# The first FFN group's work placed inside the last entry of the attention before it

## What is computed

```python
x = x + L0_xattn(ctx_1024, layernorm(x), mask)      # 8 heads of 64; q from x, k and v from context and x; l2norm of q and k
x = x + L0_ffn(layernorm(x))                        # up to 3 steps: relu(x Wm) Wp on the active quarter, top-k router
x = x + L1_xattn(layernorm(x), ctx_1024, ctx_1024)  # 16 heads of 8
x = x + L1_ffn(layernorm(x))                        # latent attention, then a mixture of 8 experts
```

## Time and profile before

| | us |
|---|---|
| median of three runs | 1278.69 |
| lowest, highest | 1275.88, 1280.52 |
| the profiled execution, whole | 1280.42 |
| its span, first to last instruction | 1278.9 |

### The profile page before, as it was taken

The page is one execution under the profiler, slowest core; times in us unless marked ns, Lnnn a source line. Parts: engine busy times, 40 slices in busy tenths (PEclk is TensorE's granted clock), DMA queues, the critical chain, the costliest instruction groups (busy, mean ns, idle before and its releaser), DMA issues.

```text
span 1278.9 us, 38214 instructions
## 1 busy us (share of the span) xinstructions
PE 1221.2 (95%) x13719; PEld 874.3 (68%) x13719; DVE 936.8 (73%) x2049; ACT 797.5 (62%) x2101; POOL 585.1 (46%) x675
## 2 busy tenths in 40 slices
PE   4899999999999995998999999999999989999996
PEld 1566666666666664447888788788888767777774
DVE  7767766777667764579999999999999965344331
ACT  2687788878877783225877787767666733333331
POOL 5476666566665663414333423353233234333442
PEclk9999999999999998998999999999999999999998
DMA  9000000000000000000000002000000000000000
GB/s 225 14 2 2 0 0 0 0 0 0 0 0 0 1 1 5 0 0 12 10 10 10 11 8 72 3 4 1 0 0 0 1 1 9 9 8 8 8 16 10
DMA packets 22742, 14.74 MB, mean 12 GB/s; under 512 B 6378, under 2 KB 21610, under 8 KB 22540
## 3 DMA queue, kind: packets, MB, share of 16 engines
q1 hardware_dynamic: 22520, 13.75, 4.3%
q10 hardware_dynamic: 148, 0.01, 0.0%
HBM read 11.66 MB, written 2.10 MB: 11 GB/s over the span
## 4 chain that ended last, share of the span: by engine, by line
PE 40%; issue 10%; POOL 5%; DVE 3%; POOLq 0%; ACT 0%; DVEq 0%
PE psum L1580 10%; PE psum L1591 5%; PE psum L1567 5%; POOL pair_acc L2310 4%; PE psum L1594 4%; PE psum L998 2%; PE psum L2090 2%; PE psum L2100 2%; PE psum L1005 2%; PE psum L1562 2%; PE psum L1546 1%; PE psum L1548 1%; PE psum L1547 1%; PE psum L1602 1%; POOL pair_acc L2304 1%
## 5 line engine op out<-in xcount | busy, mean ns | idle before, releaser
L715 POOL TENSOR_TENSOR r_norm<-ssm,mhalf 128x24 f32<-128x24 f32 x32 | 134.9, 4215 | 156.9 <-DVE ssm L619 156.8
L1948 POOL TENSOR_TENSOR pair_QX<-pair_qT,own_slots 128x512 f32<-128x512 f32 x64 | 66.6, 1040 | 248.4 <-ACT pair_qT L1679 236.0
L2156 ACT ACTIVATE pair_hid<-psum 128x512 f32<-128x512 f32 x128 | 76.4, 597 | 141.3 <-PE psum L2090 141.3
L1580 PE MATMUL psum<-ident,pair_probs 128*120 128x128 f32 (+1 forms) x1024 | 153.9, 283 | 0.4 <-ACT pair_probs L1694 0.2
L541 ACT ACTIVATE l_probs<-psum,l_n_max 128x248 f32<-128x248 f32 x256 | 117.2, 482 | 57.9 <-DVE l_n_max L637 57.9
L2310 POOL TENSOR_TENSOR pair_acc<-pair_acc,pair_prod 128x512 f32<-128x512 f32 x64 | 81.2, 1269 | 140.0 <-DVE pair_prod L2269 140.0
L1694 ACT ACTIVATE pair_probs<-psum,pair_n_max 128x120 f32<-128x120 f32 (+1 forms) x512 | 137.7, 380 | 10.8 <-DVE pair_n_max L1748 5.7
L2100 PEld LDWEIGHTS psum<-w,pair_hid 128*128 128x128 f32 x1024 | 123.1, 192 | 26.8 <-issue 26.8
L2269 DVE TENSOR_TENSOR pair_prod<-psum,pair_combine 128x512 f32<-128x512 f32 x64 | 44.2, 691 | 129.7 <-PE psum L2100 129.5
L1515 ACT COPY pair_probsT<-psum 120x512 f32<-120x512 f32 (+1 forms) x128 | 78.7, 615 | 84.7 <-PE psum L1580 84.7
L1580 PEld LDWEIGHTS psum<-ident,pair_probs 128*120 128x120 f32 (+1 forms) x1024 | 109.4, 140 | 31.1 <-ACT pair_probs L1694 12.3
(11 more groups left out here) (294 smaller groups left out, 2922.9 us busy)
## 6 DMA issues: line engine op xcount, KB each, us to landing
X<-x_in SPq DMA_DIRECT2D x8, 256.0 KB, 6.2
out_dram<-pair_acc SPq DMA_DIRECT2D x32, 64.0 KB, 1.5
CT<-ctx_in SPq DMA_DIRECT2D x8, 240.0 KB, 6.6
pair_cT<-ctxT_in SPq DMA_DIRECT2D x32, 60.0 KB, 1.8
w<-w_in SPq DMA_DIRECT2D x1, 1024.0 KB, 5.4
wm<-wm_in SPq DMA_DIRECT2D x1, 768.0 KB, 7.3
wp<-wp_in SPq DMA_DIRECT2D x1, 768.0 KB, 8.7
wkv<-wkv_in SPq DMA_DIRECT2D x1, 512.0 KB, 5.0
```

The costliest lines, as they stand in the source:

```text
L715: pool.tensor_tensor(r_norm[:, :], ssm[:, :], mhalf[:, 0:3 * H], ALU.pow).then_inc(s["norm_inverted"], 1)
L1580: tr = pe.transpose(psum[0:K, 4 + g % 2, j * P:(j + 1) * P], probs[par][:, 4 * g + j, 0:K], ident[:, :])
```

## The change

- Four `up` products, the first `down` product and the transposes (`turn_in`) of FFN group 0 stand between the steps of entry 31 of the first attention, on PE; ACT's and DVE's share of it (`copy_in`, `relu`, `load_in`, `activate`) in their bodies 30 and 31.
- Behind PE's last body `finish_first` stands: the other three `down` products of group 0, `turn_in` of group 1 and its first two `up` products. ACT copies in group 1 and copies out group 0. With that the Block ends.
- Mean and variance of entries 0 to 27 are made by DVE in body 30, the inverse roots by POOL in bodies 30 and 31. Those of entries 28 to 31 are made in the FFN's Block (`last_scales`), where DVE waits for POOL's inverse root behind group 1.
- `prepare_ffn` and its Block are gone. The joining of the weights stands on PE and ACT between the FFN and the second attention (`join_weights`), filling `history` in POOL's `make_constants`, `l1_bias` and `index` in `last_scales`. The FFN's loop on PE and DVE starts with group 2.
- `down` adds up in PSUM bank 3 in place of bank 4, since the attention uses bank 4. The context is loaded to X3, a tile that is free until the FFN writes it, in place of CT; the FFN's tiles are made ahead of the attention.

```diff
-        sem = sems.enter_context(signals(nc, "l0"))
-        CT = sb("CT", [P, B, D])
...
                 def body(n, par):
+                    last = isinstance(n, int) and n == B - 1
                     values_x(n + 1)
                     scores(n, 1, par)
                     project(n - 1)
+                    if last:
+                        pe.wait_ge(s["klT_copied"], B)
+                        pe.wait_ge(s["vc_copied"], B)
+                        ffn["turn_in"](pe, 0)
                     turn_inputs(n + 2)
                     turn_probs0(n, 0)
                     turn_probs1(n, 0)
+                    if last:
+                        pe.wait_ge(later_weights_loaded, 16 * len(later_weights))
+                        pe.wait_ge(ffn["in_copied"], 1)
+                        ffn["up"](pe, 0, 0)
                     project_kc(n + 2)
                     turn_sums(n, 0)
                     project_q(n + 2)
                     multiply_v(n, 0, par)
+                    if last:
+                        ffn["up"](pe, 0, 1)
                     turn_probs0(n, 1)
                     turn_kc(n + 1)
                     project_kl(n + 2)
                     turn_probs1(n, 1)
+                    if last:
+                        ffn["up"](pe, 0, 2)
                     turn_kl(n + 1)
                     turn_q(n + 1)
                     multiply_v(n, 1, par)
                     turn_sums(n, 1)
+                    if last:
+                        ffn["up"](pe, 0, 3)
+                        ffn["down"](pe, 0, 0)
                     values_c(n + 2)
                     scores(n + 1, 0, 1 - par)
 
                 run_steps(pe, body)
+                ffn["finish_first"](pe)
...
+                    last = isinstance(n, int) and n == B - 1
                     copy_values_c(n + 1, 1 - par)
                     exponentials(n, 0)
                     take_projection(n - 1)
+                    if last:
+                        ffn["copy_in"](act, 0)
                     make_kvT(n + 2)
                     copy_pt0(n, 0)
                     copy_values_x(n + 1, 1 - par)
                     exponentials(n, 1)
                     copy_sums(n, 0)
+                    if last:
+                        ffn["relu"](act, 0, 0)
                     copy_part(n + 2, 1, "kc_proj", "kc_copied", 6, C)
                     copy_part(n + 2, 0, "q_proj", "q_copied", 7, P)
                     copy_pt0(n, 1)
+                    if last:
+                        ffn["relu"](act, 0, 2)
                     copy_kcT(n + 1, 1 - par)
                     copy_part(n + 2, 2, "kl_proj", "kl_copied", 7, P)
                     square_qk(n + 2)
@@ -579,6 +612,8 @@
                     copy_sums(n, 1)
 
                 run_steps(act, body)
+                ffn["copy_in"](act, 1)
+                ffn["copy_out"](act, 0)
...
+                def next_variances(some):
+                    moments(dve, stats6, mean, small, next_step, some)
+                    dve.tensor_scalar(small[:, 0, some], small[:, 3, some], LN_EPS, None, ALU.add).then_inc(next_var, 1)
+
                 def body(n, par):
+                    ahead, last = (isinstance(n, int) and n == m for m in (B - 2, B - 1))
                     norm_inputs(n + 2)
                     later_stats(n)
                     maximum(n, 1)
                     invert_sums(n, 0)
                     y_moments(n - 1)
                     copy_pt1(n, 0)
+                    if ahead:
+                        dve.wait_ge(s["x_stats"], EARLY)
+                        next_variances(slice(0, EARLY))
                     scale_out(n, 0)
                     invert_sums(n, 1)
                     copy_pt1(n, 1)
+                    if last:
+                        ffn["activate"](dve, 0, 1)
                     copy_kl(n + 1, 1 - par)
                     copy_qT(n + 1, 1 - par)
                     sum_squares(n + 2)
                     y_normalize(n - 1)
+                    if ahead:
+                        dve.wait_ge(first_scaled, 1)
+                        ffn["load_in"](dve, 0)
+                    if last:
+                        dve.wait_ge(ffn["all_scales"], 1)
+                        ffn["load_in"](dve, 1)
                     maximum(n + 1, 0)
                     scale_out(n, 1)
                     x_moments(n - 2)
+                    if last:
+                        ffn["activate"](dve, 0, 3)
...
+                    if isinstance(n, int) and n == B - 2:
+                        pool.wait_ge(s["ln_made"], B)
+                        pool.wait_ge(next_var, 1)
+                        inverse_roots(pool, rstd, small[:, 0, :], mhalf, slice(0, GB)).then_inc(first_scaled, 1)
+                        inverse_roots(pool, rstd, small[:, 0, :], mhalf, slice(GB, EARLY // 2))
+                    if isinstance(n, int) and n == B - 1:
+                        inverse_roots(pool, rstd, small[:, 0, :], mhalf, slice(EARLY // 2, EARLY)).then_inc(ffn["all_scales"], 1)
 
                 run_steps(pool, body)
+                pool.iota(shared["index_i"][:, :], pattern=[[1, 8]], base=0, channel_multiplier=0).then_inc(iota_made, 1)
+                pool.wait_ge(iota_made, 1)
...
+    def finish_first(pe):
+        down(pe, 0, 1)
+        turn_in(pe, 1)
+        down(pe, 0, 2)
+        down(pe, 0, 3)
+        wait(pe, in_copied, 2)
+        up(pe, 1, 0)
+        up(pe, 1, 1)
+
+    def copy_out(act, g):
+        wait(act, multiplied[chunks - 1], g + 1)
+        wait(act, out_turned, g)
+        wait(act, out_summed, g)
+        act.copy(yT[:, :], psum[:, 3, :]).then_inc(out_copied, 1)
...
+            if begun:
+                body(1, begun=True)
+            else:
+                turn_in(pe, 0)
+                body(0, first=True)
+            ahead = 2 if begun else 1
+            with pe.Fori(0, NG - 1 - ahead) as i:
+                body(i + ahead)
             body(NG - 1, final=True)
...
+            if last_scales:
+                pool_out(0)
+                body(1)
+                last_scales()
+                dve.wait_ge(all_scales, 2)
+            else:
+                load_in(dve, 0)
+                if scales:
+                    wait(dve, all_scales, 1)
+                body(0, first=True)
+            ahead = 2 if last_scales else 1
+            with dve.Fori(0, NG - 1 - ahead) as i:
+                body(i + ahead)
             body(NG - 1, final=True)
...
+                def join_weights():
+                    pe.transpose(psum[0:LAT, 5, 0:D], mla_weights["wdkv"][:, :], ident[:, :]).then_inc(w_turned, 1)
+                    pe.wait_ge(w_copied, 1)
+                    pe.matmul(psum[:, 5, 0:D], shared["wdkvT"][:, :], mla_weights["wk"][:, :], start=True, stop=True)
+                    pe.matmul(psum[:, 5, D:2 * D], shared["wdkvT"][:, :], mla_weights["wv"][:, :], start=True, stop=True).then_inc(w_joined, 1)
+
                 def ask_router():
+                    pe.wait_ge(w_ready, 1)
...
-                    ffn["tensor"](pe, lambda: turn_input(0))
+                    ffn["tensor"](pe, lambda: turn_input(0), begun=True)
+                    join_weights()
...
-                    ffn["scalar"](act)
+                    ffn["scalar"](act, begun=True)
+                    act.wait_ge(w_turned, 1)
+                    act.copy(shared["wdkvT"][:, :], psum[0:LAT, 5, 0:D]).then_inc(w_copied, 1)
+                    act.wait_ge(w_joined, 1)
+                    act.copy(shared["joined"][:, :, :], psum[:, 5, 0:2 * D].rearrange("p (w d) -> p w d", w=2)).then_inc(w_ready, 1)
...
+                def last_scales():
+                    some = slice(B - GB, B)
+                    moments(dve, stats6, mean, small, next_step, some)
+                    dve.tensor_scalar(small[:, 0, some], small[:, 3, some], LN_EPS, None, ALU.add).then_inc(next_var, 1)
+                    dve.tensor_scalar(shared["l1_bias"][:, 0, :], shared["l1_mask"][:, :], 0.0, -2e9, ALU.is_equal,
+                                      ALU.mult).then_inc(l1_bias_made, 1)
...
+                    pool.wait_ge(next_var, 1)
+                    inverse_roots(pool, rstd, small[:, 0, :], mhalf, slice(B - GB, B)).then_inc(ffn["all_scales"], 1)
+                    make_constants(pool, router, shared, zeroed, selected, l1_bias_made)
```

260 lines of the change are left out of this document (114 added, 146 removed).

## The result

The changed kernel takes 1267.59 us (median of 4 runs, 1265.66 to 1269.06), the kernel before in the same series 1279.61 us (4 runs, 1275.88 to 1281.24). The ratio is 0.9911 with a 95% interval from 0.9892 to 0.9929: 11.4 us less, between 9.1 and 13.8. Timed a second time (experiment e1) it was 1266.94 against 1280.18 us, ratio 0.9894 [0.9875, 0.9913]. The two profiled executions have spans of 1265.5 and 1278.9 us, 13.4 us apart. The forecast was 14.8 us and 1264 us.

The account below looks back on a forecast made before the run. PE (95% busy) bounds most of the span, with an idle, half-clock hole around the first attention's end; filling it gains 16.3 - 0.5 - 1.0 = 14.8 us, so 1278.69 - 14.8 = 1263.9, say 1264 us, range 1258 to 1270.

Parts of the forecast that it names:

- (a): Between groups 1 and 2: DVE's moments, casts and wait for POOL's root cost PE 0.5 us, bounds 0 and 2.4.
- (b): Between the last `turn_back` and `project_qkv(0)`: joining the weights there delays by 1.0 us, bounds 0 and 1.5.
- Where to measure: At group 0's `turn_back`, passed by both programs: 506.6 us instead of 522.85, a gain of 16.3 us up to there.
- Entry 31 on PE: Ahead of entry 31's projection: 4.74 us of added work, 3.12 hidden in PE's gaps, so 1.6 us late.
- Entries 30 and 31 on DVE: DVE's added moments, `load_in` and relu fit its gaps in these entries: cost nothing, bounds 0 to 1.1 us.
- the sum goes by the row: For `load_in` beside POOL's roots: uses L1077's undisturbed 1.12 us, not the skill's rule allowing waits up to 2 us.
- The end of the Block: Layernorm ends at 505.0 us, PE at 505.2, together; 1.4 us later `turn_back` stands at 506.6.
- (c): POOL's constants start later, after group 1, at no cost, as POOL has nothing else until the FFN's last group.
- The clock did not fall at the FFN's start: Rival: a low-clock stretch of 10 us falls on the FFN's start, costing 5 us; time 1269 us, chance 0.12.
- the order was not held up: Rival: in entry 31 late POOL roots make `turn_in(0)` hold PE up; gain 9, time 1270 us, chance 0.07.
- the join did not cost the second attention its clock for good: Rival: PE's wait in `join_weights` keeps the second attention at the lower clock; time 1289 us, chance 0.03.
- the clock was to stay at 1.00 from 495 to 575 us: Sign in the profile after: granted clock of 1.00 from entry 31's end through the FFN, 495 to 575 us.

Follow-up runs that it names:

- e1: The changed kernel unaltered, timed again beside the kernel before: 1266.94 against 1280.18 us, ratio 0.9894.
- e2: The change without FFN work in entry 31 and without `finish_first`, against the kernel before: 1280.32 against 1280.18 us, ratio 1.0007.
- e4: The kernel before plus eight unused products in PE's waits around the Blocks' ends: 1279.53 against 1280.18 us, ratio 0.999.
- e7: The change with DVE's moments of 28 entries three steps later in body 30, behind `copy_pt1(n, 1)`; one execution: 1267.15 us.
- e9: The change with `join_weights` behind `project_qkv(0)` and POOL's constants held back until group 3's `load_in` is through; one execution: 1261.04 us.
- e5: The change with `last_scales` one group earlier, behind `pool_out(0)` instead of behind `body(1)`; one execution: 1267.84 us.
- e6: The change with `join_weights` and ACT's two copies moved behind `project_qkv(0)`, ahead of the router's first product; one execution: 1261.42 us.

## Why the prediction was right, and where its terms were off

The forecast had the direction and the size: 14.8 us less, against 11.4 (9.1 to 13.8) and 13.2 by the second timing's medians; the profiled spans differ by 13.4. The main step was right in its mechanism: PE's new work lies beside the layernorm of the last entry, and e2 shows that without it nothing of the gain is left. What is not parted by experiment is how much of it is the clock. By the rows, six instructions of `up` at 5.06 us in place of 2.58 and the `turn_in` ahead of them make some 3 us at the FFN's start, an estimate; over the whole span e4's executions allow from 3 to 7 us. That the sum of 14.8 us came as near as it did is in part luck: two errors in entry 31 cancelled, and (a) and (b) cost 3.1 us in place of 1.5, most of which the profiled execution made up for behind the FFN (12.2 us ahead at 586 us, 13.5 at the end), where the low stretches differ from one execution to the next.

The bookkeeping below compares the two profiles at equal matmul counts. After is 0.6 us behind at 453 us, ahead of any edit, a difference of the first 50 us; in other executions that starting difference was anything from 1.3 us behind to 2.5 ahead. So each place of before is set 0.59 us later where a step is measured.

- **Where to measure.** `turn_back(0)` was forecast at 506.6 us and stands at 507.13. From 522.69 + 0.59 that is 16.15 us, against 16.3 forecast (which took the chain's 522.85). The parts behind it fit as well: from the projection to PE's last end it is 505.73 - 499.94 = 5.8 us, as forecast.
- **Entry 31 on PE.** Forecast 1.6 us late; 499.94 - (497.76 + 0.59) = 1.59. But 0.54 of these are not PE's packing, they come down from entry 30 (next point). The packing cost 1.05, so PE's waits took up 3.7 of the 4.74 us where I had taken 3.12 for the most (between 489.31 and 499.94 us no row of after has any idle time before it): two errors of half a us cancelled, and that is luck.
- **Entries 30 and 31 on DVE.** I costed the moments of 28 entries at nothing, hidden in a gap of 2.01 us. They took 3.3 us (479.58 to 482.74 + 0.18) in place of 1.22, the scaling came at 482.85 instead of 481.09 + 0.59, 1.17 us late, and 0.54 of it reached PE's projection of entry 30. The step that failed is "the sum goes by the row": I had read from L1077, a `tensor_scalar` beside POOL's root, that DVE and POOL don't hold each other up, and carried it over to a `tensor_tensor` with two inputs in SBUF beside a POOL instruction that reads two inputs as well. No row that I had read showed that pair. The trace of before has one, though: at 578.78 us L932 with 8 columns took 0.42 us beside POOL's L1935 and ended with it (579.20 and 579.17), where the like L933 behind it took 0.16. In after L957 ended with L775, L958 with L794 and L964 with L799, and e7 has all three at 0.20 us or less with POOL idle. The Trainium skill ("SBUF — State Buffer", section "Who interferes with whom") says that a DVE instruction with two SBUF inputs contends with a GpSimd instruction that reads SBUF. By that sentence, which I had passed over for the one on two-port modes, the trace agrees.
- **The end of the Block.** Forecast: both chains end within 1 us of each other, and one restart of 1.4 us. DVE's last work ends at 505.49, PE's at 505.73, and the restart took 1.40.
- **(a) The scales of the last group.** Forecast 0.5 us, within 0 to 2.4. From `turn_back(0)` to `turn_back(6)` it is 554.68 - 507.13 = 47.55 us against 569.16 - 522.69 = 46.47 us before: 1.08 us, 1.05 of it in group 2. I named the moments and the wait for the root as the cause, so this step was right in its place and wrong in its cause: e9 shows that they make 0.25 us of group 2's 1.05, and POOL's memsets beside `load_in` 0.80. These are the constants that I let go at nothing in (c), because "POOL has nothing else to do": POOL had the time, but DVE paid for it. The same section of the Trainium skill ("SBUF — State Buffer", "Who interferes with whom") has `tensor_scalar` among the instructions that can shut GpSimd out, or be shut out by it; for the memsets the trace agrees (1.11 us alone, 1.90 and 3.14 beside them), for the root of 4.80 us beside L1077 it does not.
- **(b) The join.** Forecast 1.0 us, within 0 to 1.5. `project_qkv(0)` follows the last `turn_back` 1.26 us later than before (1.75 against 0.49), and `max_a(0)` another 0.74 later, 2.0 in all. In e1, e5 and e7, with the full clock there, the same distance is 5.95 us against 4.59, so the join's own price is 1.36 us; the other 0.64 is the clock that fell in after, 0.49 of it in L1621 (1.66 against 1.17 us). Moving the join (e6) brings 1.0 of the 1.36 back.
- **Behind the FFN.** The lead of after is 12.2 us at 586 us by matmul count, 15.56 (522.69 - 507.13) - 1.08 - 1.26 - 0.74 = 12.5 less 0.3 that no step names. The low stretch there was longer than before (14 against 10 us) and took 0.9 more. At 710 us the kernel before had a further low stretch, which after did not have; it gave 1.5 back. Another 0.4 came between 720 and 800 us, as in e1 and e2 too; no step names it. The row of the low stretch at 710 us, of the kernel before by stretch:

```profile
711.00:714.00 3.00, 3.00 (x44) 2.18 (x46) 1.99 (x4) 2.59 (x6) 2.68 (x4) 0.53 0.10 26
```

The change touches nothing there; e1, the change in another execution, had such a stretch at the same work. It belongs to the execution, and so does part of the difference between the 13.4 us of the profiles and the 11.4 of the medians.
- **The rivals.** The clock did not fall at the FFN's start (1.00 from 506 to 507 us), the order was not held up (`turn_in(0)` at 490.30), and the join did not cost the second attention its clock for good. One sign of the forecast came out otherwise: the clock was to stay at 1.00 from 495 to 575 us and fell at 566, which is no longer the FFN, but 5 us behind its last `turn_back`.
